# The product of state sums and gate on GpSimd for seven of eight tiles, and fewer idle products on a small constant

## The chip, the core and the metric

One core of a Trainium2 chip runs the whole program. The metric is the device time of one execution in microseconds (us); less is better. Each kernel is run several times and the median counts. One further execution is profiled, and all rows below come from it.

## What is computed

The input x has four sequences of 1024 positions and 128 channels (4096 rows). Three layers follow, each added to x:

```python
x = x + 0.5 * ffn(layernorm(x))       # 8 experts
x = x + mamba(layernorm(x))           # a selective scan
x = x + 0.5 * ffn(layernorm(x))
# ffn: every expert runs on every row
h = silu(x @ w_gate[e]) * (x @ w_up[e])          # 128 -> 512
out = sum_e cw[:, e] * (h @ w_down[e])           # 512 -> 128, cw: softmax weights of 8 experts
# mamba
xs, z = split(x @ W_in); xc = silu(conv(xs))     # 256 channels each
h = dA_t * h + dBx_t                             # 16 states, along the 1024 positions
y = sum over the 16 states of h * C_t, plus xc * D_param
out = (y * silu(z)) @ W_out                      # this product is what the change moves
```

## The kernel before

The rows are cut into eight tiles of T = 512 rows. All operands are float32; a product of large matrices is three products of rounded parts ("fp32r", lines 908, 909 and 911). `ORDER` interleaves the 16 passes of the expert layers (8 tiles, first and last layer), so that the mamba layer of a tile can run beside the expert work of others. A pass is 8 experts of 4 slots. One slot i has on **TensorE** three products for the gate, three for `up` (L908 to L911), and four float32 products of 128 columns for `down` (L1014); on **ScalarE** a silu (L1464); on **VectorE** the product of silu and `up` (L1253, "first"). In four passes at the two ends some experts are computed turned round (L1006 to L1010). A `up` product of slot i waits until VectorE has finished slot i-2 (`wt.wait_ge(S["v_h"], i - 1)`, line 987).

The mamba layer of tile t fills the gaps of the other engines. For each of 16 states VectorE makes `s_b` (L1340), two scans (L1351) and the product with C, `s_hc` (L1359). **GpSimd** then issues two DMAs that add that state to the sum Y (L1654); each waits for the landing of the one before. HS, the buffer of states, has four places, so `s_b` waits for the landing of the addition four states earlier. When all 16 have landed, `s_yz` (L1373, on VectorE) multiplies Y by SZ = silu(z). TensorE multiplies the result by W_out (`s_out`, L1072), and VectorE adds it to x (`s_add`, L1378). GpSimd also issues the additions of weighed expert outputs (L1637), and computes small vectors for the norms (L1620 to L1624) and the router (L1598 to L1615).

No engine chooses its order at run time. The function `timetable` plays the work through with estimated costs, keeps a clock for each engine, and writes a list of steps. Each engine's program goes through this list and takes its own steps in that order, with semaphores between. So a changed cost or constant in `timetable` can move steps of every engine. `LEAD` tells how far ahead of TensorE's clock VectorE's mamba work is queued; `closing` (lines 368 to 379) puts `s_yz` and, once its planned end has come, `s_out` into the list.

At the start, TensorE runs `WARM` = 3 idle products of 512 columns whose result nobody reads (L915 and L919), then four transposes of the first tile (L933, L937), one more idle product of 256 columns, and the first real products (L962, L965, L968). The idle products read HB, which VectorE sets to zero first (L1080).

Of the kernel before, what the change touches and what calls it, by code (L numbers as in the profile page):

```python
# [7 lines left out]
ALU = mybir.AluOpType  # L8
# [5 lines left out]
P = 128  # L14
T = 512
NT = 8
SUB = T // P
E = 8
# [10 lines left out]
NB = 4 - NG  # L29
HR = 4  # L30
BR = 3
WARM = 3
EPS_LN = 1e-5
# [10 lines left out]
LATE = 26  # L44
LEAD = 2.2
LAST = 2
# [11 lines left out]
TURN_SUMMED = 1.0  # L58
LANDED = 5.5
SETTLED = 2.0  # L60
SUMMED = 10.0
# [6 lines left out]
EASY = 0.4  # L68
SPLIT = 2
TURNED = [p * E + e for p in TURNS for e in TURNS[p]]  # L70
TURN_BEGINS = {p * E + TURNS[p][0]: p for p in TURNS}
TURN_ENDS = {p * E + TURNS[p][-1]: p for p in TURNS}
TURN_SUMS = {p * E + TURNS[p][-1]: p for p in TURNS if p == NPOS - 1}
TURNED_SLOTS = {g * FC + c: k * FC + c for k, g in enumerate(TURNED) for c in range(FC)}
PAIR = FC // 2
# [8 lines left out]
def timetable():  # L84
# [9 lines left out]
    def step(*what, after=0.0, **work):  # L94

        steps.append(what)
        for e, c in work.items():
            clock[e] = max(clock[e], after) + c
            after = clock[e] + SIGNAL[e]
        return after  # L100

    def give(b, sem, value, at):
        free.append((at, b, (sem, value)))
        free.sort(key=lambda f: f[0])
# [138 lines left out]
    def before(t):  # L243
# [40 lines left out]
        for j in range(2):  # L284
            bk = yield from take()
            at = step("b_dt", t, j, bk, pe=.47, a=1.1)
            give(bk[0], "a_relu", 2 * t + j + 1, at)
            yield True
# [79 lines left out]
    def closing(t):  # L368
        yield from until_v(scanned[t])
        at = step("s_yz", t, v=1.17 if t < NT - 1 else 3.5)  # L370
        yield True
        yield from until(at)
        bk = yield from take()
        at = step("s_out", t, bk, after=at, pe=1.78)
        put.add(t)
        yield from until_v(at)
        at = step("s_add", t, bk[0], after=at, v=.61)
        give(bk[0], "v_x2", t + 1, at)
        x2[t] = at
# [10 lines left out]
    def row_loads():  # L390

        while asked[0] < len(TURNED):
            g = TURNED[asked[0]]
            u = BUFFERED.index(g)
            if rows_at.get(g // E, clock["pe"]) >= clock["pe"] or (
                    u >= 2 and weighed_at.get(BUFFERED[u - 2], clock["pe"]) >= clock["pe"]):
                break
            step("cw_load", g)
            asked[0] += 1
# [184 lines left out]
def macaron_program(nc, x, W_in, conv_w, conv_b, W_x, W_dt, b_dt, A_log, D_param, W_out,  # L584
# [5 lines left out]
    with ExitStack() as ctx:  # L590
        def sb(name, shape, dt=F32):
            return ctx.enter_context(nc.sbuf_tensor(name, shape, dt))
# [20 lines left out]
        XH = sb("XH", [P, 2, 2, T], F32R)  # L613
        YE = sb("YE", [P, 2, SUB, P])
        at_hb = nc.sbuf_base
# [40 lines left out]
        for n in ("c_small c_con c_wr c_acc c_y0 c_y1 c_bcd c_dt o_x init w_hi w_lo dv "  # L656
                  "m_ct m_at a_ct a_hh v_hh a_wd v_wh v_hl v_wd v_ts v_at c_ct c_cw0 c_cw1 m_g m_u m_dn m_tr m_lg m_win m_wx m_wt m_wo m_end v_end "
                  "a_ye a_sil a_sum a_mean a_sq a_xn a_car a_lr a_xh a_exp a_neg a_rmh a_win a_tap a_yc a_dbl a_abs a_relu a_sexp a_soft a_yd a_da "
                  "v_h v_mx v_norm v_cw v_ye v_mset v_rm v_halo v_cv v_bc v_db v_sc v_hc v_yz v_x2 v_dt v_dx v_y v_wr v_lt v_xl v_ve v_nm v_xn "
                  "c_x0b m_tr0 v_mv a_sd v_x0 v_xh p_ve s_rs p_nm p_sub p_sm pl").split():  # L660
            S[n] = ctx.enter_context(nc.semaphore(n))
# [48 lines left out]
        def buffer(g):  # L710

            return YE[:, BUFFERED.index(g) % 2, :, :]

# [13 lines left out]
        def rows_loads(g):  # L727

            same = [k for k in TURNED if k <= g and (BUFFERED.index(k) - BUFFERED.index(g)) % 2 == 0]
            return f"c_cw{BUFFERED.index(g) % 2}", 16 * len(same)  # L730

# [51 lines left out]
        def wait_buffer(eng, g):  # L783

            u = BUFFERED.index(g)
            if u < 2:
                return
            last = BUFFERED[u - 2]
            if last in BY_TRANSFER:
                eng.wait_ge(S["c_acc"], 16 * added(last + 1))  # L790
            else:
                wait_weighed(eng, last)
# [108 lines left out]
        def _(pe):  # L901
# [11 lines left out]
            def idle_product(n=T):  # L913

                pe.matmul(PS[:, NG + 3, 0:n], HB[:, 0, 0:P], HB[:, 0, 0:n], start=True, stop=True)  # L915

            wt.wait_ge(S["init"], 1)
            for _ in range(WARM):
                idle_product()  # L919
            for s in steps:  # L920
# [3 lines left out]
            for s in steps:  # L924
                k = s[0]
                if k == "ln_t":
# [3 lines left out]
                    if q == 0:  # L930
                        for n, j in enumerate(FIRST_BY_VECTOR):
                            wt.wait_ge(S["v_x0"], n + 1)
                            z = pe.transpose(first_half(b, j // 2)[:, j % 2 * P:(j % 2 + 1) * P], XN[:, j, :], ident)  # L933
                            if j == SUB - 1:
                                z.then_inc(S["m_tr0"], 1)
                        wt.wait_ge(S["a_xn"], 1)
                        pe.transpose(first_half(b, 0)[:, 0:P], XN[:, 0, :], ident).then_inc(S["m_tr"], 1)  # L937
                        idle_product(2 * P)
                        continue
# [51 lines left out]
                elif k == "down":  # L991
# [6 lines left out]
                    wt.wait_ge(S[f"c_wd{e}"], 16)  # L998
                    wt.wait_ge(S["v_h"], i + 1)
                    if g in TURNED:  # L1000
                        W = WDS[:, pair(i) % 2]
# [75 lines left out]
        def _(v):  # L1077
            wt = Waits(v)
            quick = 0
            v.memset(HB[:, 0, :], 0.0).then_inc(S["init"], 1)  # L1080
            v.memset(eps[:, 0:1], EPS_LN).then_inc(S["init"], 1)
# [11 lines left out]
            for s in steps:  # L1093
# [259 lines left out]
                elif k == "s_hc":  # L1353
# [5 lines left out]
                    v.tensor_tensor(H, BCB[:, m % BR, 1, :].unsqueeze(1).broadcast_to([P, 2, T]), H, ALU.mult).then_inc(S["v_hc"], 1)  # L1359
                elif k == "s_yz":  # L1360
                    t = s[1]
# [19 lines left out]
        def _(a):  # L1381
            wt = Waits(a)
            quick = 0
            for s in steps:
# [10 lines left out]
                elif k == "ln_first":  # L1395
                    wt.wait_ge(S["init"], 2)
                    a.activation(eps[:, 1:2], eps[:, 0:1], ACT.Sqrt)
# [170 lines left out]
        def _(gp):  # L1568
# [14 lines left out]
            for s in steps:  # L1583
                k = s[0]
                if k == "ln_quick":
                    q = s[1]
                    quick += 1
                    wt.wait_ge(S["v_ve"], quick)
                    wt.wait_ge(S["init"], 5)
                    wt.wait_ge(S["a_xn"], q)  # L1590
# [25 lines left out]
                elif k == "ln_square":  # L1616
                    _, q, b = s
                    wt.wait_ge(S["a_sq"], q)
                    wt.wait_ge(S["init"], 5)
                    gp.tensor_scalar(ve[:, :], squares[:, :], 1.0 / P, EPS_LN, ALU.mult, ALU.add).then_inc(S["p_ve"], 1)  # L1620
# [4 lines left out]
                elif k == "acc":  # L1625
# [10 lines left out]
                    to = AT[:, :].rearrange("p (j d) -> p j d", j=SUB) if g in TURNED else XT[:, ORDER[p][1] % XR, :, :]  # L1636
                    gp.dma_start(to, buffer(g), accum_op=ALU.add).then_inc(S["c_acc"], 16)  # L1637
                elif k == "b_add":
                    t = s[1]
# [42 lines left out]
```

## Time and profile before

| | us |
|---|---|
| median of three runs | 1247.46 (1246.97 to 1247.85) |
| the profiled execution, its own time | 1247.65 |
| its span (first to last instruction) | 1245.7 |
| TensorE (PE) busy | 1240.6 |
| VectorE (DVE) busy | 1153.0 |
| ScalarE (ACT) busy | 996.0 |
| GpSimd (POOL) busy | 443.9 |

The profiled execution is 1.95 us longer than its span, and 0.19 us above the median. A matmul's end is modelled, so consecutive matmuls overlap in the records: their starts, not their durations, show TensorE's pace. PEld is the load of weights into TensorE. A float32 product appears as two instructions on TensorE in the trace.

### The profile page before, as it was taken

To read this page: it belongs to the slowest core of one execution; us is meant where nothing else is said; L and a number is where in the kernel's file an instruction comes from. 1 tells how busy PE (TensorE), PEld (TensorE's weight loads), DVE (VectorE), ACT (ScalarE), POOL (GpSimd) and SP (SyncE) were. 2 spreads that over 40 slices of the span, in tenths; PEclk is the share of its full clock that TensorE was granted. 3 is DMA by queue.
4 is the path that set the end of the run, shared out by engine and by line. 5 is a ranking of instruction groups with operands and counts; after the bars stand their busy time and mean duration, and the time that the engine had idled before them with its cause. 6 is when DMAs were issued, how large, how long until landed. Compare 5 with 4: busy or idle time off the path is not lost.

```text
span 1245.7 us, 20786 instructions
## 1 busy us (share of the span) xinstructions
PE 1240.6 (100%) x7232; PEld 1071.4 (86%) x7232; DVE 1153.0 (93%) x1544; ACT 996.0 (80%) x1985; POOL 443.9 (36%) x579
## 2 busy tenths in 40 slices
PE   9999999999999999999999999999999999999999
PEld 7888888888888888888888888888888888888787
DVE  5958789999999999999999999999999999999887
ACT  6678778888898888978878898788897987874654
POOL 0022133434543443543535245344443343431100
PEclk9999999999999999999999999999999999999999
DMA  8312378798869887977797798887967989894232
GB/s 230 98 28 46 84 152 172 147 198 163 162 135 201 167 173 165 187 152 157 165 207 140 156 201 182 164 173 148 194 136 165 185 174 183 165 193 80 43 63 59
DMA packets 118842, 186.71 MB, mean 150 GB/s; under 512 B 11344, under 2 KB 34000, under 8 KB 118736
## 3 DMA queue, kind: packets, MB, share of 16 engines
q0 software_dynamic: 55616, 101.47, 46.7%
q1 hardware_dynamic: 63120, 83.90, 25.3%
q8 instruction: 57, 0.93, 0.3%
q14 instruction: 49, 0.40, 0.1%
HBM read 81.20 MB, written 2.69 MB: 67 GB/s over the span
## 4 chain that ended last, share of the span: by engine, by line
PE 97%; ACT 1%; DMA 0%; DVE 0%; issue 0%; DVEq 0%; ACTq 0%
PE PS L1014 31%; PE PS L908 19%; PE PS L911 19%; PE PS L909 19%; PE PS L1010 1%; PE PS L1006 1%; PE PS L1008 1%; PE PS L1072 1%; PE PS L1057 1%; PE PS L944 1%; PE PS L952 1%; PE PS L915 0%; DMA AT<-YE 0%; PE PS L1064 0%; ACT DA L1559 0%
## 5 line engine op out<-in xcount | busy, mean ns | idle before, releaser
L1014 PEld LDWEIGHTS PS<-WD,HB 128*128 128x128 f32 x3456 | 452.4, 191 | 36.8 <-issue 1.0
L1014 PE MATMUL PS<-WD,HB 128*128 128x128 f32 x3456 | 455.7, 275 | 0.0
L1253 DVE TENSOR_TENSOR HB<-PS,HB 128x512 f32<-128x512 f32 x512 | 347.6, 679 | 60.4 <-PE PS L911 48.1
L1464 ACT ACTIVATE HB<-PS 128x512 f32<-128x512 f32 x512 | 292.8, 597 | 104.7 <-PE PS L911 100.8
L1654 POOL DMA_DIRECT2D Y<-HS x252 | 222.1, 967 | 336.2 <-DVE HS L1359 172.7
L908 PE MATMUL PS<-XH,WG 128*128 128x512 f32 x509 | 235.8, 463 | 0.0
L908 PE MATMUL PS<-XH,WU 128*128 128x512 f32 x512 | 203.8, 398 | 0.0
L911 PE MATMUL PS<-XH,WU 128*128 128x512 f32 x512 | 202.2, 395 | 0.0
L911 PE MATMUL PS<-XH,WG 128*128 128x512 f32 x509 | 200.5, 394 | 0.0
L909 PE MATMUL PS<-XH,WG 128*128 128x512 f32 x509 | 200.0, 393 | 0.0
L909 PE MATMUL PS<-XH,WU 128*128 128x512 f32 x512 | 199.9, 390 | 0.0
L1637 POOL DMA_DIRECT2D XT<-YE x107 | 102.5, 958 | 231.6 <-ACT YE L1489 103.9
L1559 ACT ACTIVATE DA<-XS,aneg 128x512 f32<-128x512 f32 x256 | 164.2, 713 | 0.8
L1351 DVE TENSOR_TENSOR_SCAN HS<-DA,car,HS 128x512 f32<-128x512 f32 x128 | 162.4, 1275 | 0.0
L1359 DVE TENSOR_TENSOR HS<-BCB,HS 128x1024 f32<-128x1024 f32 x128 | 156.0, 1219 | 1.2
L1351 DVE TENSOR_TENSOR_SCAN HS<-DA,HS 128x513 f32<-128x513 f32 x128 | 154.6, 1218 | 2.0 <-ACT DA L1559 2.0
L1340 DVE TENSOR_TENSOR HS<-BCB,DX 128x1026 f32<-128x1026 f32 (+1 forms) x128 | 155.6, 1219 | 0.6 <-DMA BCB<-BCD 0.5
L908 PEld LDWEIGHTS PS<-XH,WU 128*128 128x128 f32 x512 | 96.0, 188 | 23.2 <-issue 0.5
L909 PEld LDWEIGHTS PS<-XH,WU 128*128 128x128 f32 x512 | 96.4, 188 | 22.1 <-issue 0.5
L911 PEld LDWEIGHTS PS<-XH,WU 128*128 128x128 f32 x512 | 96.0, 188 | 22.5
L911 PEld LDWEIGHTS PS<-XH,WG 128*128 128x128 f32 x509 | 95.7, 188 | 22.3
L1464 ACT ACT_TABLE_LOAD x86 | 110.3, 1283 | 2.9 <-PE PS L911 1.3
(168 smaller groups left out, 1441.7 us busy)
## 6 DMA issues: line engine op xcount, KB each, us to landing
BCB<-BCD SPq DMA_DIRECT2D x128, 512.0 KB, 5.2
Y<-HS POOLq DMA_DIRECT2D x252, 256.0 KB, 6.3
XT<-YE POOLq DMA_DIRECT2D x107, 256.0 KB, 5.0
YE<-CWD SPq DMA_DIRECT2D x19, 256.0 KB, 4.5
AT<-YE POOLq DMA_DIRECT2D x14, 256.0 KB, 3.3
XS<-DX POOLq DMA_DIRECT2D x7, 512.0 KB, 8.6
WD<-in_L_ffn_w_down_dram SPq DMA_DIRECT2D x8, 256.0 KB, 6.2
XT<-in_L_attn_x_dram SPq DMA_DIRECT2D x7, 256.0 KB, 6.3
```

Source lines behind the costliest of these rows:

```text
L908: pe.matmul(o, w[0], m[0], start=True, stop=False)
L909: pe.matmul(o, w[1], m[0], start=False, stop=False)
L911: pe.matmul(o, w[0], m[1], start=False, stop=True).then_inc(S[sem], 1)
L1014: z = pe.matmul(part(g, j), HB[:, i % NH, j * P:(j + 1) * P], WD[:, e, c, :], start=c == 0 and j == 0, stop=c == FC - 1 and j == SUB - 1)
L1253: v.tensor_tensor(H, up(i), H, ALU.mult).then_inc(S["v_h"], 1)
L1340: v.tensor_tensor(HS[:, m % HR, :, 0:w], rows.unsqueeze(1).broadcast_to([P, 2, w]), DX[:, t % 2, :, 0:w], ALU.mult).then_inc(S["v_db"], 1)
L1351: v.tensor_tensor_scan(H, DA[:, m % NA, j, 0:w], H, car[:, j, n:n + 1] if t % 2 else 0.0, ALU.mult, ALU.add).then_inc(S["v_sc"], 1)
L1359: v.tensor_tensor(H, BCB[:, m % BR, 1, :].unsqueeze(1).broadcast_to([P, 2, T]), H, ALU.mult).then_inc(S["v_hc"], 1)
L1464: a.activation(HB[:, i % NH, :], gate(i), ACT.Silu).then_inc(S["a_sil"], 1)
L1559: z = a.activation(DA[:, m % NA, j, 0:T], XS[:, t % 2, j, 3:3 + T], ACT.Exp, scale=aneg[:, j, n:n + 1])
L1637: gp.dma_start(to, buffer(g), accum_op=ALU.add).then_inc(S["c_acc"], 16)
L1654: gp.dma_start(Y[:, t % 2, j, :], HS[:, m % HR, j, 0:T], accum_op=ALU.add).then_inc(S[f"c_y{j}"], 16)
```

## The change

Three edits reach the program; other new names (`YR`, `MARGIN`, `SPLITS`) have the value that the number they replace had, or zero.

1. `s_yz` is issued on GpSimd for tiles 0 to 6. Tile 7 stays on VectorE. In the timetable it costs GpSimd 2.4 us from VectorE's clock on, where it cost VectorE 1.17.
2. `LEAD` is 2.0 where it was 2.2.
3. The idle products read one value of `eps`, broadcast, and the zeroing of HB is gone. There are 512 + 512 + 256 columns ahead of the transposes (three times 512 before) and 128 behind (256 before).

```diff
-WARM = 3
+WARM = (T, T, T // 2)
-LEAD = 2.2
+LEAD = 2.0
...
-        at = step("s_yz", t, v=1.17 if t < NT - 1 else 3.5)
+        at = step("s_yz", t, after=clock["v"], p=2.4) if t < NT - 1 else step("s_yz", t, v=3.5)
...
-                pe.matmul(PS[:, NG + 3, 0:n], HB[:, 0, 0:P], HB[:, 0, 0:n], start=True, stop=True)
+                pe.matmul(PS[:, NG + 3, 0:n], eps[:, 0:1].broadcast_to([P, P]), eps[:, 0:1].broadcast_to([P, n]), start=True, stop=True)
...
-            for _ in range(WARM):
-                idle_product()
+            for n in WARM:
+                idle_product(n)
...
-                        idle_product(2 * P)
+                        idle_product(P)
...
-            v.memset(HB[:, 0, :], 0.0).then_inc(S["init"], 1)
             v.memset(eps[:, 0:1], EPS_LN).then_inc(S["init"], 1)
...
-                elif k == "s_yz":
+                elif k == "s_yz" and s[1] == NT - 1:
...
+                elif k == "s_yz" and s[1] < NT - 1:
+                    t = s[1]
+                    y = Y[:, t % 2, :, :]
+                    for j in range(2):
+                        wt.wait_ge(S[f"c_y{j}"], 16 * NS * (t + 1))
+                    wt.wait_ge(S["a_win"], 4 * t + 4)
+                    gp.tensor_tensor(y, y, SZ[:, t % 2, :, :], ALU.mult).then_inc(S["v_yz"], 1)
```

TensorE's queue at the start, before (L915 is the idle product, L933 and L937 the transposes, L962 the first real product):

```order
L915 MATMUL PS<-HB 128x512 x3
L933 MATMUL PS<-CON,XN 128x128 x3
L937 MATMUL PS<-CON,XN 128x128
L915 MATMUL PS<-HB 128x256
L962 MATMUL PS<-XH,WG 128x512 x3
```

The same place with the change (L919, L937, L941 and L966 are those lines of the new file):

```order
L919 MATMUL PS<-eps 128x512 x2
L919 MATMUL PS<-eps 128x256
L937 MATMUL PS<-CON,XN 128x128 x3
L941 MATMUL PS<-CON,XN 128x128
L919 MATMUL PS<-eps 128x128
L966 MATMUL PS<-XH,WG 128x512 x3
```

The order is the same, with shorter idle products. VectorE's queue around the end of tile 0's scans, before:

```order
L1359 TENSOR_TENSOR HS<-BCB,HS 128x2x512
L1253 TENSOR_TENSOR HB<-PS,HB 128x512
L1340 TENSOR_TENSOR HS<-BCB,DX 128x2x512
L1373 TENSOR_TENSOR Y<-Y,SZ 128x1024
L1253 TENSOR_TENSOR HB<-PS,HB 128x512
```

With the change the product stands in GpSimd's queue (L1650), between two additions of the next tile's states (L1667 is the old L1654, L1643 the old L1637, L1626 the old L1620):

```order
L1667 DMA Y<-HS 128x512 x2
L1650 TENSOR_TENSOR Y<-Y,SZ 128x1024
L1643 DMA XT<-YE 128x512
L1667 DMA Y<-HS 128x512 x2
L1626 TENSOR_SCALAR ve<-squares 128x4
```

The product left VectorE's queue and stands ahead of one addition of an expert's output and of the next state's two additions. Over the program VectorE loses seven such products and the zeroing and gains two weighings of an expert (L1246, from ScalarE); TensorE has the same real products as before, with `s_out` of the eight tiles behind 118, 167, 223, 271, 322, 372, 421 and 467 slots where it was 118, 168, 219, 270, 320, 372, 421 and 465.

## Rows read from the trace of the kernel before

**Rows 1.** The page: busy engines, granted clock by slices, chain that ended last

```profile
PE 1240.6 (100%) x7232; PEld 1071.4 (86%) x7232; DVE 1153.0 (93%) x1544; ACT 996.0 (80%) x1985; POOL 443.9 (36%) x579
...
PEclk9999999999999999999999999999999999999999
...
PE 97%; ACT 1%; DMA 0%; DVE 0%; issue 0%; DVEq 0%; ACTq 0%
```

**Rows 2.** Windows: length, busy us by engine, granted clock, DMA share, GB/s

```profile
280.00:1140.00 860.00, 859.44 (x5234) 753.77 (x5234) 834.98 (x1003) 720.49 (x1434) 362.94 (x453) 1.00 0.83 169
1140.00:1245.70 105.70, 102.70 (x476) 83.41 (x475) 85.83 (x173) 58.17 (x103) 11.21 (x18) 1.00 0.27 55
```

**Rows 3.** Waits of PE and its weight loads: us in total, times, longest

```profile
PE PS L1064 <- ACT XS L1532: 0.6, 2, 0.4
...
PEld PS L1064 <- ACT XS L1532: 2.2, 5, 0.8
PEld PS L1010 <- DVE HL L1209: 2.2, 7, 0.4
...
PEld PS L908 <- DVE HB L1253: 0.4, 1, 0.4
```

**Rows 4.** Timeline of the opening: start us, us, engine, line, operation

```profile
0.90 0.48 DVE L1080 MEMSET HB<- 128x512 f32 x1 [0.90 <-PEq L1669]
...
1.44 5.49 PE L915 MATMUL PS<-HB 128*128 128x512 f32 x6 [1.44 <-DVE DX L1084]
...
5.03 0.85 DVE L1121 TENSOR_SCALAR XN<-XT,mv,rs 128x128 f32<-128x128 f32 x3
...
6.72 0.75 PE L933 MATMUL PS<-CON,XN 128*128 128x128 f32 x3
...
7.31 0.27 PE L937 MATMUL PS<-CON,XN 128*128 128x128 f32 x1
...
7.42 0.60 PE L915 MATMUL PS<-HB 128*128 128x256 f32 x2
7.62 0.38 ACT L1407 ACTIVATE XH<-PS 128x256 fp32r<-128x256 f32 x1 [1.46 <-PE PS L937]
...
8.10 0.94 PE L962 MATMUL PS<-XH,WG 128*128 128x512 f32 x3
```

**Rows 5.** The idle products' line: ns min/median/max, first and last start

```profile
L915 PE MATMUL PS<-HB x8: 379/1061/1222, 1.4 to 7.6; 128*128 128x512 f32 x6, 128*128 128x256 f32 x2
```

**Rows 6.** Lines of the moved product, of GpSimd's small operations, of Y's DMAs

```profile
L1373 DVE TENSOR_TENSOR Y<-Y,SZ x8: 1210/1214/1224, 283.9 to 1137.5; 128x1024 f32<-128x1024 f32 x8
...
L1598 POOL TENSOR_TENSOR lg<-LT,mx x16: 289/590/1521, 15.3 to 1161.0; 128x64 f32<-128x64 f32 x16
...
L1605 POOL TENSOR_TENSOR z<-lg x16: 283/287/1145, 18.7 to 1162.4; 128x48 f32<-128x48 f32 x16
...
L1624 POOL TENSOR_TENSOR nm<-mean,rs x22: 198/480/1989, 65.8 to 1057.6; 128x4 f32<-128x4 f32 x22
...
DMA to landing us min/median/max: 3.3/6.3/8.7
```

**Rows 7.** Timeline near 308 and 315 us, GpSimd beside VectorE

```profile
308.99 1.10 POOL L1620 TENSOR_SCALAR ve<-squares 128x4 f32<-128x4 f32 x1 [2.76 <-ACT XN L1428]
...
308.83 1.27 DVE L1351 TENSOR_TENSOR_SCAN HS<-DA,car,HS 128x512 f32<-128x512 f32 x1
...
315.64 0.23 POOL L1607 TENSOR_TENSOR z<-z 128x24 f32<-128x24 f32 x1
...
315.41 0.66 DVE L1253 TENSOR_TENSOR HB<-PS,HB 128x512 f32<-128x512 f32 x1
```

**Rows 8.** Timeline behind tile 4's product: VectorE and TensorE

```profile
785.33 1.21 DVE L1373 TENSOR_TENSOR Y<-Y,SZ 128x1024 f32<-128x1024 f32 x1
...
794.81 0.67 DVE L1253 TENSOR_TENSOR HB<-PS,HB 128x512 f32<-128x512 f32 x1
...
796.11 0.39 PE L908 MATMUL PS<-XH,WU 128*128 128x512 f32 x1
```

More of the change, by code:

```diff
@@ L30 @@
 HR = 4
+YR = 2
 BR = 3
-WARM = 3
+WARM = (T, T, T // 2)
 EPS_LN = 1e-5
@@ L59 @@
 LANDED = 5.5
+MARGIN = 0.0
 SETTLED = 2.0
@@ L69 @@
 SPLIT = 2
+SPLITS = {0: range(2, 6), 1: range(1, 5), 14: range(4, 8), 15: range(0, 7)}
 TURNED = [p * E + e for p in TURNS for e in TURNS[p]]
+SPLIT_EXPERTS = [p * E + e for p in SPLITS for e in SPLITS[p]]
 TURN_BEGINS = {p * E + TURNS[p][0]: p for p in TURNS}
@@ L73 @@
 TURN_SUMS = {p * E + TURNS[p][-1]: p for p in TURNS if p == NPOS - 1}
-TURNED_SLOTS = {g * FC + c: k * FC + c for k, g in enumerate(TURNED) for c in range(FC)}
+TURNED_SLOTS = {g * FC + c: k * FC + c for k, g in enumerate(SPLIT_EXPERTS) for c in range(FC)}
 PAIR = FC // 2
@@ L286, in before @@
             at = step("b_dt", t, j, bk, pe=.47, a=1.1)
-            give(bk[0], "a_relu", 2 * t + j + 1, at)
+            give(bk[0], "a_relu", 2 * t + j + 1, at + MARGIN)
             yield True
@@ L395, in row_loads @@
             if rows_at.get(g // E, clock["pe"]) >= clock["pe"] or (
-                    u >= 2 and weighed_at.get(BUFFERED[u - 2], clock["pe"]) >= clock["pe"]):
+                    u >= YR and weighed_at.get(BUFFERED[u - YR], clock["pe"]) >= clock["pe"]):
                 break
@@ L613, in macaron_program @@
         XH = sb("XH", [P, 2, 2, T], F32R)
-        YE = sb("YE", [P, 2, SUB, P])
+        YE = sb("YE", [P, YR, SUB, P])
         at_hb = nc.sbuf_base
@@ L656, in macaron_program @@
         for n in ("c_small c_con c_wr c_acc c_y0 c_y1 c_bcd c_dt o_x init w_hi w_lo dv "
-                  "m_ct m_at a_ct a_hh v_hh a_wd v_wh v_hl v_wd v_ts v_at c_ct c_cw0 c_cw1 m_g m_u m_dn m_tr m_lg m_win m_wx m_wt m_wo m_end v_end "
+                  "m_ct m_at a_ct a_hh v_hh a_wd v_wh v_hl v_wd v_ts v_at c_ct c_cw0 c_cw1 c_cw2 m_g m_u m_dn m_tr m_lg m_win m_wx m_wt m_wo m_end v_end "
                   "a_ye a_sil a_sum a_mean a_sq a_xn a_car a_lr a_xh a_exp a_neg a_rmh a_win a_tap a_yc a_dbl a_abs a_relu a_sexp a_soft a_yd a_da "
@@ L710, in buffer @@
         def buffer(g):
-            return YE[:, BUFFERED.index(g) % 2, :, :]
+            return YE[:, BUFFERED.index(g) % YR, :, :]
         def flat(ap):
@@ L727, in rows_loads @@
         def rows_loads(g):
-            same = [k for k in TURNED if k <= g and (BUFFERED.index(k) - BUFFERED.index(g)) % 2 == 0]
-            return f"c_cw{BUFFERED.index(g) % 2}", 16 * len(same)
+            same = [k for k in TURNED if k <= g and (BUFFERED.index(k) - BUFFERED.index(g)) % YR == 0]
+            return f"c_cw{BUFFERED.index(g) % YR}", 16 * len(same)
         def wait_high(eng, i):
@@ L785, in wait_buffer @@
             u = BUFFERED.index(g)
-            if u < 2:
+            if u < YR:
                 return
-            last = BUFFERED[u - 2]
+            last = BUFFERED[u - YR]
             if last in BY_TRANSFER:
@@ L999, in _ @@
                     wt.wait_ge(S["v_h"], i + 1)
+                    if g in TURNED and i not in TURNED_SLOTS:
+                        pe.matmul(turned(g), WD[:, e, c, :], HB[:, i % NH, :], start=c == 0, stop=c == FC - 1).then_inc(S["m_dn"], 1)
+                        continue
                     if g in TURNED:
@@ L1395, in _ @@
                 elif k == "ln_first":
-                    wt.wait_ge(S["init"], 2)
+                    wt.wait_ge(S["init"], 1)
                     a.activation(eps[:, 1:2], eps[:, 0:1], ACT.Sqrt)
@@ L1588, in _ @@
                     wt.wait_ge(S["v_ve"], quick)
-                    wt.wait_ge(S["init"], 5)
+                    wt.wait_ge(S["init"], 4)
                     wt.wait_ge(S["a_xn"], q)
@@ L1618, in _ @@
                     wt.wait_ge(S["a_sq"], q)
-                    wt.wait_ge(S["init"], 5)
+                    wt.wait_ge(S["init"], 4)
                     gp.tensor_scalar(ve[:, :], squares[:, :], 1.0 / P, EPS_LN, ALU.mult, ALU.add).then_inc(S["p_ve"], 1)
```

## The prediction
> **What bounds the kernel now.** I read the page first, then windows, then the list of waits, then two pieces of timeline. The page has TensorE busy for 1240.6 of 1245.7 us and 97% of the chain that ended last on it, at the full clock in every slice [rows 1]. From 280 to 1140 us it is busy for 859.4 of 860 [rows 2]. As ends are modelled, a full row of busy time does not exclude short waits, so I looked at what the weight loads, which run just ahead of the products, wait for: 2.2 us for ScalarE ahead of L1064, 2.2 us for VectorE ahead of L1010, 0.4 us for VectorE ahead of L908, and on the product side 0.6 us [rows 3]. That is about 5 us in the whole program in which another engine held TensorE back. The same number of real products has to be done after the change. So TensorE bounds it, and what any edit can win is what lies ahead of the first real product (8.10 us, [rows 4]), these 5 us, and nothing else.
>
> VectorE is the next engine: 835 of 860 us in the middle [rows 2], yet TensorE hardly ever waits for it there. Taking 1.2 us from it seven times frees an engine that is nearly full but not the last.
>
> **Edit 1, the opening.** Removed: the zeroing of HB, 0.48 us from 0.90 on, for whose end the idle products waited; the next memsets are 0.06 us, so the first idle product can start at about 1.02 where it started at 1.44 [rows 4]: 0.42 us. The idle products were six instructions of 512 columns in 5.49 us; the last lasts 1.06 [rows 5], so they start (5.49 - 1.06) / 5 = 0.89 us apart. The new ones are four such and two of half the length, five in all: 0.89 us less. Together TensorE would be free for the transposes 1.31 us earlier, at 5.41 where L933 started at 6.72. The rows that it transposes were ready before that: VectorE's three end at 5.88, some 0.28 us apart [rows 4]. So two transposes can go at once and the third waits for 5.88 and the signal, to about 5.95; the fourth follows at about 6.2 where it was at 7.31. That is 1.1 us. Behind it the chain is as before: ScalarE's copy L1407 (its inputs waited 1.46 us for PE), then L962. ScalarE's L1394 and the weights are not in the way by the same view, which has no DMA wait there. The last idle product was 0.60 us in 7.42 to 8.02 and is now half as long, so it ends before L962 even at half the clock. I take **-1.1 us**.
>
> The unknown here is TensorE's clock. 512 columns took 0.89 us an instruction up to 6.7 us, and 256 columns start (0.60 - 0.38) = 0.22 us apart at 7.42 [rows 4, 5]: per column 1.7 ns and then 0.9 ns, that is the 1.2 GHz and then the 2.4 GHz level. Before it rose, the engine had worked without a break since 1.44. It now starts earlier, and works without a break until about 6.7, then waits some 0.3 us for its first operands. If the rise comes at the same time as before, or earlier, the first real products are at the full clock. If it comes later, nine products of 512 columns (L962, L965, L968) go at half of it. Three of them take (0.94 - 0.40) / 2 = 0.27 us each now; I price the loss at 0.2 us for each, 1.8 us in all. So the bounds of this term are -1.3 (all of it) and +0.7 (1.1 won, 1.8 lost).
>
> **Edit 2, the product on GpSimd.** VectorE loses 7 x 1.21 = 8.5 us [rows 6], and TensorE does not wait for it in the middle, so directly this is worth nothing. What it can change is the 2.6 us that TensorE's loads wait for VectorE [rows 3], and most of that is in the turned passes at the ends, where no `s_yz` stands (tile 0's is at 283.9, [rows 6]). I give 0.1 us.
>
> What it costs GpSimd has no row: no operation of it has 1024 elements. The nearest are 289 ns for 64, 283 for 48 and 198 for 4 elements at their shortest [rows 6]. From 4 to 64 elements that is 1.5 ns an element, from 4 to 48 it is 1.9. So I estimate 0.2 + 1024 x 1.5 to 1.9 = 1.75 to 2.2 us, near the 2.4 of the timetable, far from its origin. The Trainium skill's GPSIMD Engine Reference (3.1 Elementwise) has 4497 ns for a 2048-element `tensor_tensor` against 2293 on VectorE, and makes VectorE the rule; half of it is an estimate of 2.25 us, and no run here shows that figure.
>
> Queued behind it on GpSimd are the addition of a weighed expert and the next state's two additions. They come up to 2.2 us later. The state's addition lands 6.3 us after its issue [rows 6], and `s_b` asks for it four states later, which is over 25 us in this stretch (16 states in some 120 us), so nobody notices. `s_out` on TensorE is the one that can: in the order it stands up to four slots later or one earlier than before. The product starts as soon as the last addition has landed, when GpSimd gets to it; on VectorE it stood in a full queue. 0.0 us, with a bound of 7 x 0.3 if it comes late each time.
>
> The other cost is the meeting of the two engines. In the rows a GpSimd operation of 4 elements, issued at 308.99 while VectorE's scan ran, took 1.10 us and ended at 310.09, within 0.02 us of the scan's end; another of 24 elements beside VectorE's L1253, one of whose inputs is in PSUM, took 0.23 [rows 7]. L1624 takes from 198 up to 1989 ns for the same work [rows 6]. So GpSimd waits here for VectorE's operations with two operands in SBUF. The other way round no row shows, as GpSimd's operations are all too short. The lower bound is that VectorE loses nothing; the upper that it stands still for the whole of the new operation, 2.2 us. Against the 1.21 that it no longer spends, it would then be 1.0 us later for a while at each of seven places. Behind tile 4's product the closest reading is L1253 ending at 795.48 and the `up` product that waits for it starting at 796.11, 0.63 us later [rows 8]; at the other tiles the least that I found in the 14 us behind is 2.1, 0.9, 1.0, 1.1, 1.1 and 1.9 us. So even the upper bound costs TensorE some 0.5 us in all. I take **+0.2 us**, nearer to the lower end, since VectorE's L1253 every 2.3 us gives way to GpSimd.
>
> The Trainium skill's page "SBUF — State Buffer" (Who interferes with whom) is stricter: a VectorE instruction with two SBUF inputs and a GpSimd one that reads SBUF exclude each other, and the second stands still for the whole of the first. By that rule the sum would have the upper bound, 0.5 us in place of 0.2. The trace agrees for GpSimd as the second; for VectorE as the second no row shows it.
>
> **Edit 3, the order.** `LEAD` and the new costs move steps of all engines by a few places, but TensorE's products are the same, and `s_out` is 0 to 4 slots off. I take -0.2 us of the 5 us of waits; it could be -2.5 (most of them gone) or +0.5.
>
> **Sum.** 1247.65 (profiled execution) - 1.1 - 0.1 + 0.2 - 0.2 = 1246.45. The median of the runs is 0.19 below that execution, so 1246.3.
>
> **The rivals.** *The clock rises late.* Nine real products at half the clock: 1247.65 + 0.7 - 0.1 = 1248.25, as a median 1248.1. For it: two idle products fewer in length. Against it: TensorE starts earlier, works on until 6.7, and has only a short gap.
>
> *The new order takes the waits away.* The loads ahead of L1010 and L1064 wait 4.4 us in twelve places [rows 3], which a queue of VectorE with 8.5 us less in it and less of mamba work ahead could shorten. 1247.65 - 1.1 - 2.5 = 1244.05, as a median 1243.9, faster. Against it: L1064 waits for ScalarE, which the change does not relieve.
>
> *VectorE stands still longer than the spare time behind it.* If each blocks the other in turn, the GpSimd operation is stretched too. With 3.4 us (2.2 and one VectorE operation of 1.2), VectorE is 2.2 us late at each of seven tiles. Less the spare times above, this is 0.1 + 1.3 + 1.2 + 1.1 + 1.6 + 1.1 + 0.3 = 6.7 us: 1246.3 - 0.2 + 6.7 = 1252.8, slower. It decides from about 2.5 us of standstill on. For it: the 1989 ns of L1624; VectorE has only 3% idle time in the middle to catch up. Against it: half of VectorE's neighbours there are L1253, during which GpSimd can read.
>
> **How the numbers follow.** I give the forecast 0.60, the late clock 0.10, the vanished waits 0.18, the standstill 0.12. About 0.2% (2.5 us) is what a measurement of this kernel can tell from no change: faster is below 1245.0, slower above 1250.0. The first two cases are no change, 0.70; the third is faster, 0.18; the fourth slower, 0.12. The range goes down to 1243.9, the third case, and up to 1249.2, past the late clock and into the smaller sizes of the standstill.
>
> **What the profile after would show.** L962 at about 7.0 us in place of 8.10, with the three of it still in 0.94 us; if they take over 1.2, the clock was late. The product as a row of POOL with 1.7 to 2.4 us, seven times; over 3 us would mean that it is held up. VectorE's operations with two SBUF operands at 1.21 to 1.28 us: a longest one of 2 us or more, or a start that late beside the product, is the standstill. VectorE busy for about 1145 us. The waits of PEld ahead of L1010 and L1064 near 4.4 us. I am wrong in the reasoning, even with the right number, if L962 has not moved, and wrong in the bound if TensorE's busy time in 280 to 1140 us has gaps of over 2 us.

## The result and the profile after

The changed kernel takes **1259.34 us** (median of five runs, 1258.68 to 1260.96) against 1247.46 before: a ratio of 1.0098 with a 95% interval of 1.0087 to 1.0109, so 12 us slower. The predicted 1246.3 us and its range up to 1249.2 were both wrong. The profiled execution took 1260.2 us, with a span of 1258.4.

The page after, with the busy time of each engine, the granted clock by slices and the chain that ended last, the lines that stand against [rows 1]:

```profile
PE 1244.4 (99%) x7232; PEld 1071.4 (85%) x7232; DVE 1157.4 (92%) x1538; ACT 994.3 (79%) x1977; POOL 466.8 (37%) x586
...
PEclk9999999999999999999999999999999999999999
...
PE 85%; ACT 4%; DMA 4%; DVE 3%; issue 3%; POOL 1%; DVEq 0%; SPq 0%; ACTq 0%; POOLq 0%
```

Two things are off at once. The chain was 97% TensorE and is 85% TensorE. And VectorE lost 7 x 1.21 us of work and the zeroing and gained two weighings (0.68 us each), but its busy time rose by 4.4 us. Windows after, which stand against [rows 2] (the columns are the same; the second window is longer as the span is):

```profile
280.00:1140.00 860.00, 852.40 (x5170) 743.25 (x5169) 828.73 (x986) 715.13 (x1419) 384.06 (x458) 1.00 0.82 168
1140.00:1258.40 118.40, 113.06 (x533) 92.66 (x531) 96.55 (x185) 60.52 (x108) 12.31 (x19) 0.99 0.26 53
```

TensorE is idle for 7.6 us of the middle 860, where it was idle for 0.6. The waits, which stand against [rows 3] (us in total, times, longest):

```profile
PEld PS L912 <- DVE HB L1259: 7.1, 12, 2.0
PEld PS L1017 <- DVE HL L1215: 4.7, 6, 2.8
...
DVE YE L1195 <- DMA YE<-CWD: 3.0, 1, 3.0
PE PS L912 <- DVE HB L1259: 3.0, 4, 1.6
...
PE PS L1017 <- DVE HL L1215: 2.4, 1, 2.4
```

L912, L1017 and L1259 are the old L908, L1010 and L1253. Two waits have grown: that of the `up` product for VectorE's L1259 (0.4 us on the weight loads before, 7.1 now), and that of the turned pass at the end (2.2 us before, 4.7 now; longest 0.4 before, 2.8 now). The row of L1195 is new: VectorE itself waits 3.0 us for a DMA.

The first of the two has its origin in these rows, the lines of the product (L1650) and of the scan (L1357, before L1351), with shortest, median and longest time in ns:

```profile
L1650 POOL TENSOR_TENSOR Y<-Y,SZ x7: 2419/2714/3408, 283.3 to 1038.4; 128x1024 f32<-128x1024 f32 x7
...
L1357 DVE TENSOR_TENSOR_SCAN HS<-DA,HS x128: 1195/1216/3724, 150.6 to 1021.6; 128x513 f32<-128x513 f32 x128
L1357 DVE TENSOR_TENSOR_SCAN HS<-DA,car,HS x128: 1250/1272/4371, 277.7 to 1142.8; 128x512 f32<-128x512 f32 x128
```

A scan that takes 1.27 us in the median took 4.37 once. The timeline at three of the seven products (start us, us):

```profile
539.75 3.41 POOL L1650 TENSOR_TENSOR Y<-Y,SZ 128x1024 f32<-128x1024 f32 x1
539.88 4.37 DVE L1357 TENSOR_TENSOR_SCAN HS<-DA,car,HS 128x512 f32<-128x512 f32 x1
...
662.60 1.19 POOL L1667 DMA_DIRECT2D Y<-HS  x1
663.16 3.05 POOL L1650 TENSOR_TENSOR Y<-Y,SZ 128x1024 f32<-128x1024 f32 x1
663.58 3.72 DVE L1357 TENSOR_TENSOR_SCAN HS<-DA,HS 128x513 f32<-128x513 f32 x1
...
908.80 2.68 POOL L1650 TENSOR_TENSOR Y<-Y,SZ 128x1024 f32<-128x1024 f32 x1
909.62 0.69 DVE L1259 TENSOR_TENSOR HB<-PS,HB 128x512 f32<-128x512 f32 x1 [1.19 <-PE PS L915]
910.23 2.35 DVE L1357 TENSOR_TENSOR_SCAN HS<-DA,HS 128x513 f32<-128x513 f32 x1
```

Each scan begins while GpSimd is at work and ends 1.09 to 1.10 us after GpSimd's end (539.75 + 3.41 = 543.16 and 544.25; 666.21 and 667.30; 911.48 and 912.58). A scan takes 1.22 to 1.27 us by itself, so it makes next to no headway while GpSimd computes. L1259, one of whose operands lies in PSUM, runs through in its usual 0.69 us inside the third product. Over the seven places the VectorE operations that meet a product are longer than usual by 2.6, 0.2, 3.1, 2.5, 1.8, 1.1 and 2.9 us, 14.2 in all: more than the 8.5 us that were taken off VectorE.

The product itself is not stretched in these rows, though its records are 2.42 to 3.41 us long. The record of the second product begins while GpSimd still issues the DMA ahead of it (662.60 + 1.19 = 663.79), and ends 2.42 us after that issue. The other products of this trace end 2.40 to 2.42 us after the issue ahead of them too, or, where none is close, are 2.42 us long.

The second stands at the end of the program:

```profile
1191.55 0.69 DVE L1195 TENSOR_TENSOR YE<-PS,YE 128x512 f32<-128x512 f32 x1 [3.00 <-DMA YE<-CWD]
...
1193.49 0.50 PE L1017 MATMUL PS<-HL,WDS 128*128 128x512 f32 x1 [2.41 <-DVE HL L1215]
...
1194.53 0.60 PE L912 MATMUL PS<-XH,WU 128*128 128x512 f32 x1
1194.93 0.63 PE L913 MATMUL PS<-XH,WU 128*128 128x512 f32 x1
```

VectorE waits for the weights of the experts, which SyncE stores and reads back (`CWD`); TensorE waits 2.41 us for VectorE; and from 1194.53 on eight products start 0.42 us apart (1194.53 to 1197.91) where the ones just ahead of them were 0.23 apart. The windows show the clock that goes with it:

```profile
1188.00:1194.00 6.00, 3.59 (x16) 2.65 (x15) 2.96 (x7) 1.68 (x3) 0.85 (x1) 1.00 0.34 87
1194.00:1199.00 5.00, 5.00 (x17) 3.88 (x17) 2.56 (x6) 2.42 (x4) 0.00 (x0) 0.66 0.43 86
1199.00:1204.00 5.00, 5.00 (x26) 4.15 (x25) 3.79 (x7) 2.80 (x6) 0.00 (x0) 1.00 0.28 69
```

The granted clock averages 0.66 over the 5 us behind the pause, that is the 1.2 GHz level for 3.4 of them (5 x 0.34 x 2) and the 2.4 GHz level for the rest. The wait and the lower clock together cost about 2.4 + 8 x 0.2 = 4 us here.

The opening went nearly as predicted. Its timeline, against [rows 4]:

```profile
0.91 4.63 PE L919 MATMUL PS<-eps 128*128 128x512 f32 x6 [0.91 <-DVE DA L1089]
...
5.49 0.90 PE L937 MATMUL PS<-CON,XN 128*128 128x128 f32 x3
...
7.12 0.94 PE L966 MATMUL PS<-XH,WG 128*128 128x512 f32 x3 [0.18 <-ACT XH L1413]
```

The first real product starts at 7.12 us where it started at 8.10, and three of them still take 0.94 us. How much of that is the edit is asked below (e3).

### The profile page after: what moved, and what is told of

Read it like the earlier page. It is cut to its first block, busy times and chain, and to the rows that moved or that the text cites. A ratio compares the mean times of both kernels' runs of the same rounds, so it can differ in the third digit from the quotient of the medians.

```text
span 1258.4 us, 20786 instructions
## 1 busy us (share of the span) xinstructions
PE 1244.4 (99%) x7232; PEld 1071.4 (85%) x7232; DVE 1157.4 (92%) x1538; ACT 994.3 (79%) x1977; POOL 466.8 (37%) x586
## 4 chain that ended last, share of the span: by engine, by line
PE 85%; ACT 4%; DMA 4%; DVE 3%; issue 3%; POOL 1%; DVEq 0%; SPq 0%; ACTq 0%; POOLq 0%
PE PS L1021 26%; PE PS L912 17%; PE PS L915 17%; PE PS L913 17%; DMA Y<-HS 4%; PE PS L1017 1%; PE PS L1013 1%; PE PS L1015 1%; PE PS L1064 1%; DVE HB L1259 1%; PE PS L1079 1%; ACT DA L1565 1%; DVE HS L1357 1%; PE PS L948 1%; ACT L1565 1%
## 5 line engine op out<-in xcount | busy, mean ns | idle before, releaser
L1259 DVE TENSOR_TENSOR HB<-PS,HB 128x512 f32<-128x512 f32 x512 | 346.6, 678 | 72.0 <-PE PS L915 56.7
L1667 POOL DMA_DIRECT2D Y<-HS x252 | 223.7, 981 | 320.1 <-DVE HS L1365 165.3
L912 PE MATMUL PS<-XH,WG 128*128 128x512 f32 x509 | 235.4, 463 | 0.4 <-ACT HB L1470 0.4
L912 PE MATMUL PS<-XH,WU 128*128 128x512 f32 x512 | 205.0, 400 | 3.0 <-DVE HB L1259 3.0
L915 PE MATMUL PS<-XH,WU 128*128 128x512 f32 x512 | 202.2, 395 | 0.0
L915 PE MATMUL PS<-XH,WG 128*128 128x512 f32 x509 | 200.7, 394 | 0.0
L1643 POOL DMA_DIRECT2D XT<-YE x107 | 103.2, 964 | 227.3 <-DVE YE L1252 135.9
L1357 DVE TENSOR_TENSOR_SCAN HS<-DA,car,HS 128x512 f32<-128x512 f32 x128 | 169.2, 1337 | 0.0
L1357 DVE TENSOR_TENSOR_SCAN HS<-DA,HS 128x513 f32<-128x513 f32 x128 | 158.1, 1245 | 3.8 <-ACT DA L1565 3.8
L912 PEld LDWEIGHTS PS<-XH,WU 128*128 128x128 f32 x512 | 96.1, 188 | 29.1 <-DVE HB L1259 7.1
L915 PEld LDWEIGHTS PS<-XH,WU 128*128 128x128 f32 x512 | 96.2, 188 | 22.7
L915 PEld LDWEIGHTS PS<-XH,WG 128*128 128x128 f32 x509 | 95.8, 188 | 22.2
```

The costliest lines, as they stand in the source:

```text
L912: pe.matmul(o, w[0], m[0], start=True, stop=False)
L915: pe.matmul(o, w[0], m[1], start=False, stop=True).then_inc(S[sem], 1)
L1259: v.tensor_tensor(H, up(i), H, ALU.mult).then_inc(S["v_h"], 1)
L1357: v.tensor_tensor_scan(H, DA[:, m % NA, j, 0:w], H, car[:, j, n:n + 1] if t % 2 else 0.0, ALU.mult, ALU.add).then_inc(S["v_sc"], 1)
L1667: gp.dma_start(Y[:, t % 2, j, :], HS[:, m % HR, j, 0:T], accum_op=ALU.add).then_inc(S[f"c_y{j}"], 16)
```

## The experiments

Two theories stood at the start of the experiments: (a) VectorE stands still beside GpSimd's product, and that is the loss; (b) the new order of steps is the loss. A third was that the opening does not gain what its rows show. Each kernel is timed beside runs of the kernel before on the same chip; the ratio is to those.

**e1: the changed kernel with the product back on VectorE, at the same steps.**

```diff
-                elif k == "s_yz" and s[1] == NT - 1:
+                elif k == "s_yz":
...
-                elif k == "s_yz" and s[1] < NT - 1:
...
-                    gp.tensor_tensor(y, y, SZ[:, t % 2, :, :], ALU.mult).then_inc(S["v_yz"], 1)
```

> The changed kernel with its order of steps, but the seven products are issued by VectorE again. Theory (standstill): in the changed kernel a scan on VectorE beside GpSimd's product took 3.9 and 4.4 us where it takes 1.27, so the loss comes from the meeting of the two engines. Then this kernel is back near 1246.5 us (1247.5 less 1.0 for the opening), at most 1248, and the longest scan is under 1.5 us. Rival (order): the new places of the steps cause the waits of TensorE. Then it stays at 1257 to 1260. If both have a part, the time in between shares it out.

Measured: 1254.91 us, ratio 1.0062 (1.0045 to 1.0079). More than half of the loss is there without any product on GpSimd. The waits in its profile:

```profile
PEld PS L1017 <- DVE HL L1215: 5.2, 8, 3.1
...
DVE YE L1195 <- DMA YE<-CWD: 3.3, 1, 3.3
...
PEld PS L912 <- DVE HB L1259: 1.6, 3, 0.7
```

The late `CWD` is here too, while the wait for L1259 is 1.6 us instead of 7.1. So the two waits have two causes. VectorE is busy for 1151.7 us here and for 1157.4 in the changed kernel: 5.7 more, which is the 14.2 us of standing still less the 8.5 us of products.

**e2: the kernel before, only the engine of the seven products changed (the timetable still plans 1.17 us of VectorE for each).**

```diff
-                elif k == "s_yz":
+                elif k == "s_yz" and s[1] == NT - 1:
...
+                elif k == "s_yz" and s[1] < NT - 1:
...
+                    gp.tensor_tensor(y, y, SZ[:, t % 2, :, :], ALU.mult).then_inc(S["v_yz"], 1)
```

> The kernel before, timetable and opening untouched; only the engine that issues the seven products is GpSimd. Standstill: slower, 1252 to 1259, with seven scans or sums on VectorE of 3 us or more. Order: 1247.5, as all steps stand where they stood. Here the order was planned with VectorE's 1.17 us for the product, so TensorE may also wait at the output product, up to 1.5 us each time.

Measured: 1256.01 us, ratio 1.0071 (1.0056 to 1.0086). With the old order the product costs 9 us, but for another reason, the first row below from the waits and the others from the timeline:

```profile
PE PS L1072 <- POOL Y L1644: 6.0, 3, 2.6
```

```profile
410.17 3.01 POOL L1644 TENSOR_TENSOR Y<-Y,SZ 128x1024 f32<-128x1024 f32 x1
...
413.32 1.91 PE L1072 MATMUL PS<-WO,Y 128*128 128x128 f32 x15 [2.56 <-POOL Y L1644]
```

`s_out` stands where a product of 1.17 us would be done. These 6.0 us are nearly all that the profiled execution lost (1253.76 us, the shortest of the four; its span is 6.3 us longer than before). VectorE does stand still, by 10.1 us in all: three of its operations take over 3 us (3.13, 3.86 and 4.09), two take 2.50 and 2.77, and at two of the seven places none is held, so "seven of 3 us or more" was wrong. But the weight loads wait 0.4 us for L1253, as before: at the old places, where the prediction had read the spare times, they were enough. In the changed kernel, which plans 2.4 us, TensorE never waits for GpSimd's product: that part of the change is right and needed.

**e3: the kernel before with the new opening alone** (`WARM`, the operand of the idle products, no zeroing of HB).

> The kernel before with the shorter idle products on the small constant alone. Both theories: 1.0 us less than before, 1246.4 to 1246.6, L962 at 7.1 us in place of 8.1, and no further difference behind it.

Measured: 1246.55 us over 10 runs, ratio 0.9999 (0.9989 to 1.0008): no difference that can be told. Its timeline says why the 1.1 us don't arrive in full:

```profile
4.05 0.29 DVE L1100 BATCH_NORM_STATS2 stats<-XT 128x6 f32<-128x128 f32 x1 [0.65 <-DMA XT<-in_L_attn_x_dram]
...
7.56 0.93 PE L962 MATMUL PS<-XH,WG 128*128 128x512 f32 x3 [0.30 <-ACT XH L1406]
```

In this execution part of x landed later, and the chain through VectorE and ScalarE set the start of L962: 7.56, not 7.12. TensorE is now free early and waits for x. The same start in all twelve profiles shows no gain at all. With the old opening it is 8.10 (before), 7.54 (e2), 6.92 (e4), 7.22 (e7) and 7.06 us (e8); with the new one 7.12 (after), 7.71, 7.56, 6.94, 7.46, 6.96 and 7.73 us (e1, e3, e5, e6, e9, e10). The means are 7.37 and 7.35. In the profile of before, the idle products start 0.85 us apart to their end; in e4 the last of them start 0.43 apart, so the clock was already at its higher level, and the transposes began at 5.70, not 6.72.

**e4: the kernel before with LEAD 2.0 alone.**

> The kernel before with LEAD 2.0 in place of 2.2 alone. Standstill: 1247 to 1249, since nothing meets anew. Order: a good part of the 12 us, 1252 or more, since this constant moves the mamba steps of every tile.

Measured: 1263.1 us, ratio 1.0131 (1.0116 to 1.0146), worse than the whole change. Its timeline has single waits that [rows 3] does not:

```profile
774.14 1.23 DVE L1351 TENSOR_TENSOR_SCAN HS<-DA,HS 128x513 f32<-128x513 f32 x1 [4.88 <-ACT DA L1559]
...
777.46 0.79 PE L908 MATMUL PS<-XH,WU 128*128 128x512 f32 x1 [4.01 <-DVE HB L1253]
...
1171.91 3.65 PE L1072 MATMUL PS<-WO,Y 128*128 128x128 f32 x16 [4.89 <-DVE Y L1373]
```

A scan waits 4.88 us for ScalarE's decays, which come too late in this order; L1253 stands behind the scan in VectorE's queue, and TensorE waits for it. The longest single wait is the third row: TensorE waits 4.89 us at the last tile's output product for `s_yz`. No wait for `CWD` is among this run's.

**e5 and e6: the changed kernel with LEAD 2.2, with the product on GpSimd (e5) and on VectorE (e6).** The first edit is that of e5; e6 has it and that of e1.

```diff
-LEAD = 2.0
+LEAD = 2.2
```

> The changed kernel with LEAD back at 2.2; the product stays on GpSimd. The constant alone cost 16 us in the kernel before. If the constant also stands behind the changed kernel's order, this one is at 1250 to 1253 (standstill only, 4.4 us, on an order as good as before). If any change of the timetable's inputs gives an order that is worse by some us, it is anywhere from 1252 to 1265.

> The same with the product issued by VectorE at the same steps. The difference to the run before it is the price of the product on GpSimd in this order: 3 to 6 us by the standstill, as 4.4 us in the changed kernel's order. Its own distance from the kernel before is the price of this order: 0 to 1 us if LEAD was the cause, 5 us or more if the cost given to the product in the timetable moves as much.

Measured: e5 1254.43 us, ratio 1.0049 (1.0032 to 1.0066); e6 1248.41 us over 10 runs, ratio 1.0007 (0.9998 to 1.0017). These two differ in nothing but the engine of the product: 6.0 us, at the upper end of the 3 to 6 that were expected; the order costs 1.1 us with the old LEAD, where 0 to 1 was expected. The wait that goes with the product, on the weight loads and on TensorE itself, from e5 and from e6:

```profile
PEld PS L912 <- DVE HB L1259: 10.3, 13, 4.1
PE PS L912 <- DVE HB L1259: 5.8, 5, 3.7
```

```profile
PEld PS L912 <- DVE HB L1259: 3.0, 4, 1.2
PE PS L912 <- DVE HB L1259: 1.4, 2, 0.7
```

One place in the timeline of e5 shows how VectorE's standstill reaches TensorE:

```profile
897.37 4.17 DVE L1357 TENSOR_TENSOR_SCAN HS<-DA,HS 128x513 f32<-128x513 f32 x1 [1.36 <-ACT DA L1565]
897.80 2.64 POOL L1650 TENSOR_TENSOR Y<-Y,SZ 128x1024 f32<-128x1024 f32 x1
...
901.46 1.26 DVE L1259 TENSOR_TENSOR HB<-PS,HB 128x512 f32<-128x512 f32 x2
902.17 0.71 PE L912 MATMUL PS<-XH,WU 128*128 128x512 f32 x1 [3.69 <-DVE HB L1259]
```

and the window behind it (columns as in [rows 2]):

```profile
902.00:906.00 4.00, 3.83 (x16) 3.55 (x17) 2.84 (x5) 3.97 (x6) 0.00 (x0) 0.57 0.01 4
```

The scan stands still, and L1259 behind it in VectorE's queue cannot pass it. The `up` product, which needs L1259 of two slots before, waits 3.69 us, and the clock is at its lower level for 3.4 of the next 4 us (4 x 0.43 x 2), in which half the work is done: 1.7 us lost. With the 4.4 us by which TensorE's waits for L1259 grew (5.8 against 1.4) that comes to about 6 us.

Neither e5 nor e6 has a wait for `CWD`. Only after and e1 have it, which plan 2.4 us of GpSimd and have LEAD 2.0; e4, with LEAD 2.0 and the old plan, has not. The last `CWD` store is issued later in every run with LEAD 2.0 (1186.4 us in after, 1182.0 in e1, 1201.5 in e4) than with 2.2 (1173.7 before, 1168.0 in e5, 1162.2 in e6).

**e7 and e8: is it the reading?** The kernel before, with the product still on VectorE, and GpSimd given one extra operation on 1024 elements at the same seven places. In e7 it multiplies parts of two weight tensors, in e8 it only writes zeros; both write into a buffer that is idle then.

```diff
+                elif k == "s_yz" and s[1] < NT - 1:
+                    t = s[1]
+                    for j in range(2):
+                        wt.wait_ge(S[f"c_y{j}"], 16 * NS * (t + 1))
e7 +                 own(gp.tensor_tensor(HI[:, 0:2, :], WG[:, 0, 6:8, :].bitcast(F32), WU[:, 0, 6:8, :].bitcast(F32), ALU.mult))
e8 +                 own(gp.memset(HI[:, 0:2, :].bitcast(F32), 0.0))
```

> The kernel before, with one more GpSimd product of 1024 elements at each of the seven places, from two constant weight tiles into a buffer that is idle there; the real product stays on VectorE and nobody waits for the extra one. Standstill: VectorE operations with two SBUF operands that meet it last until its end plus their own length (3.5 us and more), about 2.5 us lost at each of seven places, less the spare time of 0.6 to 2.1 us: 1250 to 1253 us. Order alone: 1247, since no step moves and nothing waits.

> As the run with the extra product, but the extra operation is a memset of the same 1024 elements, which reads nothing. If it is the reading of SBUF that stops VectorE: no VectorE operation over 1.4 us and 1246.5 to 1247.5 us. If any GpSimd operation does it, or the delay of GpSimd's queue costs the time: as slow as the run with the product.

Measured: e7 1252.77 us, ratio 1.0042 (1.0027 to 1.0057); e8 1247.28 us over 10 runs, ratio 1.000 (0.9991 to 1.0010). Both are within what was expected. No engine waits for the extra operation's result, none of the order is changed, and the reading operation costs 5.5 us where the writing one costs nothing. The memset is also shorter (0.95 us at its shortest, against 2.67 for the product), so the two times alone do not separate reading from length; the rows do. The timeline of e7 and then of e8 at the same place, where VectorE's instruction begins inside GpSimd's:

```profile
282.42 3.05 POOL L1642 TENSOR_TENSOR HI<-WG,WU 128x1024 fp32r<-128x1024 f32 x1
282.93 3.63 DVE L1373 TENSOR_TENSOR Y<-Y,SZ 128x1024 f32<-128x1024 f32 x1
```

```profile
282.17 1.64 POOL L1642 MEMSET HI<- 128x1024 f32 x1
282.69 1.22 DVE L1373 TENSOR_TENSOR Y<-Y,SZ 128x1024 f32<-128x1024 f32 x1
```

3.63 us against 1.22 for the same VectorE instruction. In e8 VectorE's scans never exceed 1.29 us; in e7 one takes 2.98. This isolates (a). Part of e7's loss is that the real `s_yz` stands still and `s_out` waits for it (2.1 us on TensorE, none before), so e7 shows the cause, not its price in the changed kernel.

**e9: the product in four pieces.** The changed kernel with LEAD 2.2 (e5), where the product is issued as four instructions of 256 elements. Left out of the diff are the counts of the two waits for `v_yz`, which rise by four a tile.

```diff
...
-                    gp.tensor_tensor(y, y, SZ[:, t % 2, :, :], ALU.mult).then_inc(S["v_yz"], 1)
+                    for j in range(2):
+                        for h in range(2):
+                            cols = slice(h * T // 2, (h + 1) * T // 2)
+                            z = gp.tensor_tensor(y[:, j, cols], y[:, j, cols], SZ[:, t % 2, j, cols], ALU.mult)
+                            z.then_inc(S["v_yz"], 1)
```

> The changed kernel with LEAD back at 2.2 and GpSimd's product cut into four pieces of 256 elements, each issued as an instruction of its own. Theory (VectorE's two-operand instructions and GpSimd's stand still for one another): a piece should hold VectorE for at most about 0.75 us, so that the longest scan beside one is about 2.1 us instead of 3.7, and the groups of waits on HB shrink; but each piece may itself wait for a VectorE instruction, so that the product is done up to about 8 us after its start instead of the planned 2.4, and s_out may wait for it. If the harm comes from the length of one hold, the time is 1249 to 1252, nearer to e6 (1248.4) than to e5 (1254.4). If it comes from the summed time of the holds, or the late product now stops s_out, it is 1254 to 1258.

Measured: 1257.06 us, ratio 1.0082 (1.0065 to 1.0098), no better than e5 and probably worse (1.0049; the intervals just touch). That the hold would be cut to one piece is refuted by its timeline:

```profile
1032.82 3.32 POOL L1653 TENSOR_TENSOR Y<-Y,SZ 128x256 f32<-128x256 f32 x4
1033.26 3.97 DVE L1357 TENSOR_TENSOR_SCAN HS<-DA,car,HS 128x512 f32<-128x512 f32 x1
```

The scan did not get in between the pieces. They followed one another at once, it waited for all four, and ended 1.09 us after the last. So it was at six of the seven places. At the other one (404.64 us) a scan ended 1.09 us after the third piece, and the fourth took 1.64 us instead of 0.7. The pieces end 0.67 to 0.70 us after one another, so four of them take 2.8 us where one instruction takes 2.4; from first start to last end they took 3.05 to 3.73 us, against 2.39 to 3.27 in e5. The product never came up to 8 us after its start.

**e10: LEAD on the other side.** The kernel of e3 with LEAD 2.4.

> The kernel before with the new opening (as e3) and LEAD 2.4 instead of 2.2; the product is VectorE's. Two theories of what LEAD does. If a LEAD below 2.2 costs because less mamba work queued ahead leaves VectorE, ScalarE and TensorE closer to each other, more of it helps or does nothing: 1244 to 1247. If 2.2 is only the value for which this timetable happens to fit, and any other moves steps so that a few of them come late, it costs in this direction too: 1249 to 1262, with single waits of 1 us or more of TensorE that the kernel before does not have. I expect the second.

Measured: 1274.89 us, ratio 1.0202 (1.0163 to 1.0242), with runs from 1267.99 to 1282.02. The direction was as expected, the size beyond it. One wait carries 14.7 of the 34.5 us by which the profiled execution (1282.02 us) is above the kernel before on that chip, from its timeline:

```profile
1188.46 1.22 DVE L1372 TENSOR_TENSOR Y<-Y,SZ 128x1024 f32<-128x1024 f32 x1
...
1189.83 3.50 PE L1072 MATMUL PS<-WO,Y 128*128 128x128 f32 x16 [14.74 <-DVE Y L1372]
```

The last tile's product, which ended the mamba work at 1137.5 before [rows 6], starts 51 us later, and TensorE, whose order is fixed, stands in front of its output product. It is the place where e4 waits 4.89 us. So 2.2 is not "enough lead": of the three values tried it is the one at which this timetable fits, and 0.2 to either side puts some steps in the wrong place.

## Why the prediction was wrong

From the kernel before to the changed one, in the order e6, e5, after: 1.1 + 6.0 + 4.9 = 12.0 us by the medians (0.9, 5.2 and 6.1 by the ratios, as not all ran on one chip), where 12 were measured. In the order e6, e1, after it is 1.1 + 6.5 + 4.4. So the product on GpSimd is 4.4 to 6.0 us of it, LEAD 4.9 to 6.5, all else about 1. LEAD's share holds for the new plan alone: with the old one the same constant costs 16 us (e4).

- **What bounds it.** Right and the reason for the rest: TensorE had 5 us to win and everything to lose. That its busy time in the middle would fall short of full by over 2 us was named as the sign of being wrong, and it is 7.6.
- **The opening, -1.1 us.** As a reading of one profile it came out: idle products at 0.91 (said 1.02), transposes at 5.49 (5.41), L966 at 7.12 (about 7.0), clock up in time. The step that failed is that TensorE's idle products hold the transposes. They did in the profile of before, which has the latest start of five with the old opening; in the other four the clock rose earlier (between 4.7 and 6.1 us, not at 7.2), and the mean starts of the old and the new opening are equal (7.37 and 7.35 us). The median of e3 is 0.3 us lower, within its noise. No gain is shown.
- **The cost of the product itself.** 1.75 to 2.2 us was the estimate, and at its shortest it takes 2.39 us (e5). The Trainium skill's GPSIMD Engine Reference (3.1 Elementwise), halved, gave 2.25, the nearer figure. Records of over 3 us were to mean that it is held up. Those of the changed kernel (3.05, 3.08 and 3.41) do not: they include the end of the DMA issue ahead of the product. Held by a scan it was once in e2 and once in e7, at places where no such issue stood just ahead: both times it ended 2.18 us after the scan.
- **The standstill, +0.2 us with an upper bound of 0.5.** This is the first step that failed, worth 4.4 to 6.0 us. The failure has two parts. First, "The other way round no row shows" was taken for a reason to stay near the lower end. It was a gap in what the trace could show, and the Trainium skill's "SBUF — State Buffer" (Who interferes with whom) filled it: the second of the two stands still for the whole of the first. The runs agree with that rule in most that they touch: L1259 with a PSUM operand is not stopped, the memset of e8 is harmless, and the scan, two of whose operands are in SBUF, stops. Which of the two counts as the first they leave open: the scan of e5 shown above began 0.43 us before GpSimd's product and still stood still. It was the same at 1038.05 us of the changed kernel and at one place each of e2 and e7 (0.20 to 0.35 us before); at all four GpSimd was then issuing the DMA just ahead of the product. Second, the price of the rule was too low. "1.0 us later for a while", checked against spare times at the old places, held for the old places: e2 has no more waits for L1253 than the kernel before. It left out that a scan in front of L1259 becomes up to 3.1 us longer where only 1.21 was taken away, and that new places have other spare times: e5 waits 3.69 us at one of them alone, and pays another 1.7 us in clock behind it. The rival that priced a hold of 3.4 us came to 6.7 us for this term, near the 6.0 of e5 against e6, but it spread the loss over all seven old places, where e2 shows none of it, and had no term for the clock: the nearness of the number is in part luck. The rival still deserved more than 0.12.
- **Order and LEAD, -0.2 us with bounds of -2.5 and +0.5.** The second step that failed, worth 4.9 to 6.5 us, and outside its bounds. The reasoning looked at TensorE's own steps ("`s_out` is 0 to 4 slots off") and at waits that could vanish. A wait that does not exist in the trace of before had no price there, and such a one decided: `CWD` stored too late for the turned pass, 3.0 us of VectorE, 2.4 of TensorE, then 3.4 us at the lower clock, 4 us in all. Most of the rest are waits of TensorE at L948 (the old L944), 2.2 us in after and 1.5 in e1, which neither e5 nor e6 has. Edits of LEAD alone cost 16 us (e4) and 27 us (e10), so an upper bound of +0.5 was far too low.
- **The rest.** Nothing queued behind the product was noticed, and no wait of TensorE for it exists after the change, as predicted. The clock did not rise late in the opening. The loads' waits at L1071 and L1017 (the old L1064 and L1010), said to stay near 4.4 us, are 2.8 and 4.7.

What is left open: which step of the timetable moved `CWD`'s store behind the point where VectorE needs it. The runs show that the engine of the product has no part in it, as e1 has it too, and that the wait needs both LEAD 2.0 and the new plan. Open is also what decides which of VectorE's and GpSimd's instructions stands still.

## To carry to other kernels

Beside an almost full VectorE, an operation moved to GpSimd relieves nothing if it reads SBUF: it stops VectorE's instructions with two SBUF operands until it has ended, here for up to 3.1 us where 1.21 was taken away. Beside VectorE work with an operand in PSUM, or as an operation that only writes, it took nothing from VectorE here; that moving it would then pay no run shows. Cutting it up does not help if the pieces follow one another. Where an order is worked out from constants, a trace of the old order bounds what an edit of a constant can win, but not what it can lose; only a run prices it. And a gain read from the first microseconds of one profile wants a second profile of the old kernel: the start of the first real product varied by over 1 us between profiles with the same opening.

## What the runs showed of the hardware

- A GpSimd instruction on 1024 float32 elements per partition with two SBUF operands takes 2.39 us at its shortest, one on 256 elements 0.7, and a memset of 1024 elements 0.95. Their records begin up to 1 us before the DMA issue ahead of them on GpSimd has ended, and are longer by that.
- VectorE's instruction with two SBUF operands that begins during such a product ends 1.08 to 1.10 us after it (25 of 28 products in after, e2, e5 and e7), and also after four shorter ones in a row. Beside a memset it takes its usual 1.22.
- Twice (e2, e7) VectorE's scan was ahead, took its usual 1.22 us, and the product ended 2.18 us after it.
- A pause of 2.4 us of TensorE near the end of the program was followed by 3.4 us at the 1.2 GHz level, in which products start 0.42 instead of 0.23 us apart, and one of 3.7 us in e5 likewise. Pauses of 2.6 and 2.4 us in e2 were not followed by any. The page's slices of 31 us show none of it.
